# When VectorE transposes the mask of the next chunk in a masked graph attention kernel

## The reference

```python
h = jnp.maximum(_layernorm(x, axis=-1), 0.0)
h1 = h @ a[:d]
h2 = h @ a[d:]
e = leaky_relu(h1 + h2.T, negative_slope=0.01)
attention = softmax(where(adj > 0, e, NEG_BIG), axis=1)
out = x + attention @ h
```

## Time and profile before

| | us |
|---|---|
| median of three runs | 1551.02 |
| lowest, highest | 1548.48, 1551.06 |
| the profiled execution | 1552.08 |
| its span | 1550.3 |
| TensorE matmul, busy | 1522.7 (98%) |
| VectorE, busy | 1489.6 (96%) |
| ScalarE, busy | 1162.5 (75%) |
| GpSimd, busy | 457.4 (30%) |

### The profile page before, as it was taken

How to read it: one execution, slowest core, us unless ns; L and a number is a source line. 1 busy time by engine, 2 the same in 40 slices (tenths; PEclk the granted TensorE clock), 3 DMA queues, 4 the chain that set the end, 5 groups by cost and what they waited for, 6 DMA issues and landing times.

```text
span 1550.3 us, 38852 instructions
## 1 busy us (share of the span) xinstructions
PE 1522.7 (98%) x12678; PEld 1511.9 (98%) x12678; DVE 1489.6 (96%) x2172; ACT 1162.5 (75%) x1180; POOL 457.4 (30%) x547
## 2 busy tenths in 40 slices
PE   5999999999999999999999999999999999999999
PEld 5999999999999999999999999999999999999998
DVE  7999999999999999999999999999999999999998
ACT  7787877778777777677776876777777777677774
POOL 6363334335452340120420320320320320420420
PEclk9999999999999999999999999999999999999999
DMA  6666677787778799999999999999999999999994
GB/s 211 222 200 230 206 223 227 230 248 221 245 220 254 220 225 233 221 201 206 218 207 207 224 204 207 226 197 210 230 195 205 228 195 207 217 195 209 219 199 98
DMA packets 436493, 331.05 MB, mean 214 GB/s; under 512 B 16704, under 2 KB 378176, under 8 KB 436416
## 3 DMA queue, kind: packets, MB, share of 16 engines
q1 hardware_dynamic: 411360, 288.94, 83.6%
q10 hardware_dynamic: 25056, 41.13, 8.7%
HBM read 308.90 MB, written 21.10 MB: 213 GB/s over the span
## 4 chain that ended last, share of the span: by engine, by line
PE 82%; DMA 5%; DVE 3%; ACT 3%; issue 2%; SPq 1%; ACTq 0%; DVEq 0%
PE acc L950 27%; PE acc L953 26%; PE acc L952 26%; DMA adj_in<-in_adj_dram 5%; PE T L917 2%; ACT mask L542 2%; DVE w_lo L797 1%; DVE halves L786 1%; SPq L268 1%; ACT w_hi L552 0%; DVE T L767 0%; DVE w_lo L801 0%; ACT w_hi L555 0%; DVE adj_in L901 0%; DVE adj_in L896 0%
## 5 line engine op out<-in xcount | busy, mean ns | idle before, releaser
L950 PE MATMUL acc<-h_hi,w_hi 128*128 128x258 f32 (+1 forms) x4096 | 1167.3, 285 | 9.2 <-DVE w_lo L801 3.4
L953 PE MATMUL acc<-h_hi,w_lo 128*128 128x258 f32 (+1 forms) x4096 | 1153.3, 282 | 0.0
L952 PE MATMUL acc<-h_lo,w_hi 128*128 128x256 f32 (+1 forms) x4096 | 1149.7, 281 | 0.0
L950 PEld LDWEIGHTS acc<-h_hi,w_hi 128*128 128x128 f32 x4096 | 771.8, 188 | 17.8 <-issue 8.0
L952 PEld LDWEIGHTS acc<-h_lo,w_hi 128*128 128x128 f32 x4096 | 778.4, 190 | 0.1
L953 PEld LDWEIGHTS acc<-h_hi,w_lo 128*128 128x128 f32 x4096 | 775.3, 189 | 0.0
L786 DVE SCALAR_TENSOR_TENSOR halves<-r_rep,g_all,T 128x512 f32<-128x512 f32 (+1 forms) x1024 | 712.7, 736 | 10.8 <-PE T L917 1.5
L542 ACT ACTIVATE mask<-adj_in,mhalf 128x2048 fp8e5<-128x2048 int32 x256 | 510.3, 1993 | 58.8 <-DMA adj_in<-in_adj_dram 58.5
L552 ACT ACTIVATE w_hi<-halves 128x1024 fp32r<-128x1024 f32 x336 | 353.6, 1057 | 185.0 <-DVE halves L786 172.3
L797 DVE SCALAR_TENSOR_TENSOR w_lo<-halves,w_hi 128x1024 fp32r<-128x1024 f32 x336 | 418.2, 1245 | 9.9 <-PE acc L953 4.9
L555 ACT ACTIVATE w_hi<-halves 128x1024 fp32r<-128x1024 f32 x176 | 185.3, 1057 | 97.5 <-DVE halves L786 92.6
(11 more groups left out here) (70 smaller groups left out, 343.8 us busy)
## 6 DMA issues: line engine op xcount, KB each, us to landing
adj_in<-in_adj_dram SPq DMA_DIRECT2D x672, 256.0 KB, 5.0
adj_in<-in_adj_dram SPq DMA_DIRECT2D x88, 1024.0 KB, 6.3
part_sums<-stage ACTq DMA_DIRECT2D x24, 516.0 KB, 5.6
xo<-part_sums ACTq DMA_DIRECT2D x24, 516.0 KB, 4.4
r_rep<-r_rows SPq DMA_DIRECT2D x39, 256.0 KB, 4.8
xb<-in_x_dram ACTq DMA_DIRECT2D x15, 512.0 KB, 5.9
out_dram<-xb ACTq DMA_DIRECT2D x15, 512.0 KB, 4.7
xb<-in_x_dram SPq DMA_DIRECT2D x14, 512.0 KB, 5.8
```

What stands on the lines that cost most here:

```text
L950: nc.tensor.matmul(acc[:, t, 0:WC], w_hi[:, k % HL, cols], rhs_hi, start=start and u == 0, stop=False)
L952: nc.tensor.matmul(acc[:, t, 0:D], w_hi[:, k % HL, cols], rhs_lo, start=False, stop=False)
L953: last = nc.tensor.matmul(acc[:, t, 0:WC], w_lo[:, k % LL, cols], rhs_hi, start=False, stop=stop and u == 1)
```

## The change

On VectorE the transpose of the mask of a chunk moves from the front of the chunk's own work to the chunk before, in front of the weights of its second pair (k = 1 or k = 3), after the subtraction. The condition takes the kind of the chunk that it transposes for: at the end of a visit (`last`, kc = 1) that is `V.dt_next`. The last step of all has no next chunk (`V.tail`). The other engines are untouched.

```diff
-            def transpose_mask(V, n, kc):
+            def transpose_mask(n, kc, dt):
 
                 g = n * CI + kc
-                t = G - V.dt
-                if V.dt < G:
+                t = G - dt
+                if dt < G:
                     dve.wait_ge(s_T, g + 1)
                 else:
                     dve.wait_ge(s_mask, g + 1)
...
                     else:
-                        if V.dt and k % 2 == 0:
-                            transpose_mask(V, n, kc)
                         if not (isinstance(V.v, int) and V.v == 1 and first and k < 2):
                             subtract(g - 2, (k + 2) % 4, True, V.deep and not (enter and k < 2))
+                        dt = V.dt_next if last and kc == 1 else V.dt
+                        if dt and k % 2 == 1 and not (V.tail and last and kc == 1):
+                            transpose_mask(n + (kc + 1) // CI, (kc + 1) % CI, dt)
                         if first:
                             side_work(V, k)
                         if second:
```

## The result

The changed kernel takes 1561.62 us (median of four runs, 1560.06 to 1562.38) against 1549.99 for the kernel before (four runs, 1548.48 to 1551.06). The ratio is 1.0067, 95% interval 1.0052 to 1.0081: slower, by 8 to 13 us. The forecast was slower, 1565, with a range of 1556 to 1577. The profiled spans are 1560.6 and 1550.3.

A forecast was written before the change was run, and what follows sets the result against it. TensorE bounds the kernel, VectorE hardly faster. Three undisturbed pairs of visits (4.2 us) plus five late-load groups (10.0) add 14.2 us to the profiled 1552.1: 1566.3, so 1565 as median; range 1556 to 1577.

The forecast's parts named there:

- The bound, and the lead: TensorE bounds, VectorE catches up 0.2 us per chunk; lead is subtraction's end to its first matmul, 0.45 behind an evacuation.
- (a): Undisturbed chunks: the second weights come 0.63 to 0.65 us later, hidden by VectorE's own work; cost nothing.
- (b): VectorE's mask wait moves ahead of the second weights (1.31 us), delaying them and the next subtraction; 1.22 us behind evacuations.
- The second evacuation, and the pair: Late mask four chunks on the pair's second visit costs 0.48 us; with the first's 0.92, 1.40 per undisturbed pair.
- returns elsewhere: Shared SBUF port: a subtraction's 0.54 us GpSimd slowdown goes at one place, returns at others; under 4 us on the sum.
- The late loads: Conversions waiting for late loads, five groups: each costs TensorE 1.1 to 2.9 us, taken 2.0; 10.0 us in all.
- The low end of the range: Each late-load group 1.1 us, three pairs 4.2: +9.7, down to +5 if loads catch up while TensorE waits.
- The rival of the load queue: SyncE's loads, issued later, bunch less with evacuation transfers; some 12 us regained, 1549; chance of faster 8%.
- one of the two signs of being wrong: VectorE's transpose waits grow but matmul counts don't, or conversions' waits for loads fall well below 57.5 us.
- The ring: Mask, transpose, weights, rounding, conversion form a loop of 5.6 to 6.1 us with scaling; lateness persists, +28, 1579; chance 14%.
- What would show it: VectorE's waits at the transpose go from 6.7 to 35 to 45 us; evacuation stretches lose some 12 matmuls.
- The part up to 560 us: The stretch of the kernel up to 560 us was claimed to stay unchanged.

The follow-up runs named there:

- wait_only: Kernel before, transpose at its old place, but VectorE also waits for the next chunk's mask ahead of the second weights; ratio 1.0066 to the kernel before.
- thin_share: Changed kernel with GpSimd's two operations for empty rows on 8 of 256 columns; ratio 1.0045 to the kernel before.
- light_before: Kernel before with x reload and output store in the last 80 steps cut to one tile of four; ratio 0.9961 to the kernel before, 1545.01 us.
- light_after: Changed kernel with x reload and output store in the last 80 steps cut to one tile of four; ratio 1.0069 to the kernel before, 1561.74 us.
- hold_before: Kernel before with SyncE issuing one load of each eight-step visit 2.2 us later; ratio 1.0031 to the kernel before.
- old_first: Changed kernel with the transpose for the chunk after a visit's first step at its old place; ratio 1.0021 to the kernel before.
- behind_s1: Kernel before with the transpose moved behind the chunk's first subtraction, ahead of its first weights; ratio 1.0093 to the kernel before.

## Why the prediction was right, point by point

The direction and the mechanism were right: the wait ahead of W2 costs, behind the evacuations. That the time came out within 3.4 us of the forecast is partly luck. The forecast added 14.2 us: 4.2 for three undisturbed pairs and 10.0 for late loads. The measured spans differ by 10.3: 5.7 for these pairs, 3.4 for the others and 1.1 ahead of them, which no term foresaw. One term was too small, the other too large by far.

- **The bound, and the lead.** TensorE's pace and VectorE's small reserve were read rightly. The lead of 0.45 of which 0.30 may go gave a stall of 0.92 us behind an evacuation; against the trace before, the chunk behind the evacuation starts 0.93 to 0.95 us later in each of the seven pairs from the second on. The forecast had counted it in three only.
- **(a) W2 later costs nothing.** Right: wait_only leaves undisturbed W2 in place and is as slow, and in the changed kernel the last nine chunks of an undisturbed pair lose nothing with W2 later in each.
- **(b) The wait ahead of W2.** Right, and by wait_only nearly the whole of the cost. Predicted wait of VectorE behind the evacuation 1.22 (from a start that would overlap), listed 1.14; S1 comes 1.21 later.
- **The second evacuation, and the pair.** Predicted 1.40 a pair, measured 1.85 to 1.92. Two steps were off. The second evacuation was priced at 0.48 "with the lead already used"; in the kernel before S1 still had a lead of 0.38 there (over at 883.48, first matmul at 883.86), of which 0.23 could go, and the chunk behind it loses 0.31 to 0.33. The larger one is the slow S. I took it that S1 moves out of GpSimd's way and gains 0.54 a visit. It did, but another S (872.83, 1.70 us) moved into GpSimd's way between the two evacuations, and one behind the second that is slow in both kernels (ten chunks into the pair) now finds less lead (0.41 us; 0.58 in the kernel before). That is the part of the skill's rule that I had set beside the sum ("returns elsewhere"); thin_share, in which all S are quick, shows its price, 0.4 us a pair. Its pairs 3 to 7 lie 1.42 to 1.45 above those of light_before: near 1.40, with other parts than predicted. Three pairs came to 5.7 us instead of 4.2.
- **The late loads.** The term that was mis-sized: 5 x 2.0 = 10.0 us predicted, 3.4 measured (0.8 + 2.2 + 0.9 - 0.8 + 0.3), and these 3.4 hold the evacuations' stalls of the five pairs too. I added the late wait on top of loads as late as before, and let it override the evacuation's 0.92. It was the other way round: the stalls of the evacuations came in every pair from the second on, and covered the loads. The landing was taken to move 0.9 us with its issue, and did (0.6 to 1.2 in the undisturbed pairs); what was not seen is that its use moves further. In the changed kernel ScalarE's conversions after the evacuation come about 2 us later against TensorE (chunk 141: 19.9 us after the start of chunk 136, before 17.9) while the load lands at 16.4 (before 15.7). So the loads are no longer last there. The low end of the range had named this ("if late loads get time to catch up while TensorE waits"). light_before and light_after show it: only the kernel before has anything to gain from fewer bytes.
- **The rivals.** The rival of the load queue had the effect right (waits for loads well below 57.5) and the cause wrong: not loads that bunch less, since a load held back lands later (hold_before), but, as far as the runs show, a backlog that the standstills pay off. It won back some 5 us of the 12 named, not the 10 from which it would have decided. With the fall to 9.7 us one of the two signs of being wrong that the prediction named did appear, and it was right about the part that it concerns: the loads. The ring did not show: the pairs heal within their ten steps, and the leads are those of the kernel before (within 0.05 us) from chunk 147 on, six chunks behind the second evacuation.
- **What would show it.** The waits at the transpose were to be 35 to 45 us, and are 21.0: of the two kinds only the one behind evacuations came in full, fourteen waits in pairs 2 to 8, 1.14 us behind a first evacuation and 0.66 to 0.74 behind a second. Matmuls missing in the stretch with a pair's evacuations: some 12 predicted, 12 measured from 850 to 900 us (422 before, 410 after), 10 from 950 to 1000 (424, 414), and 16 over the whole pair from 954 to 1068.
- **The part up to 560 us** was to be unchanged. Of the 10.3 us of the spans, 1.1 stand there, where the order didn't change. They arise in the first two chunks and stay to 0.1 us for the next 500 us. The six traces with VectorE's old order and no added wait reach the first late chunk at 576.1 to 576.6 us of their spans, six of the eight others at 577.2 to 577.6, the last two at 575.1 and 576.2. It goes with the program more than with the execution; what in it does this is open.

## What to carry to other kernels

A wait in an in-order queue costs what is queued behind it, not what it waits for: before moving a wait ahead of an operation, set the end of what it waits for against the new place chunk by chunk, above all behind the irregular work (here the evacuations), and subtract the lead that the bounding engine still has there. Two causes that stall the same engine don't add up: a stall taken out in one place lets late transfers show in another (old_first), and one put in can hide them (light_before and light_after). So undisturbed periods and sums are to be compared, not single late spots. An operation that could fill time between a writer and its reader is worth its place there even when it seems free to move.

## What the runs showed of the hardware that was not expected

- VectorE starts an operation that reads the result of the one just before it (weights behind the transpose into PSUM that they read, behind_s1) 0.75 us after that one's start in 104 of 168 cases and 0.87 to 0.89 after in the 64 of the hardware loop; an independent one starts 0.63 after (all 168 in the changed kernel, to 0.01). The dependence costs 0.12 us, in the loop 0.25. Over a chunk (5.66 or 5.78 against 5.50, where TensorE needs 5.70) this decided between catching up, keeping up and falling behind.
- A subtraction with both inputs in SBUF was stretched from 1.22 to 1.70 us where a GpSimd operation had begun 0.12 us before it. The same holds over all 14 traces: 273 subtractions that began while a GpSimd tensor_tensor (L410, L419, L426) had more than 0.2 us left took as long as it still ran plus 1.08 us, to 0.03. Where the GpSimd operation had begun at most 0.05 us before the subtraction, it could be the other way round: in 102 cases the subtraction took its usual time and the GpSimd operation 1.5 us or more instead of 0.7. The Trainium skill ("SBUF — State Buffer", section "Who interferes with whom") says that such a VectorE instruction contends with a GpSimd instruction that reads SBUF. The trace agrees for these operations. It shows no such stretch beside L423, a tensor_scalar with its input in SBUF: 306 subtractions began while it was the one running, with more than 0.2 us to go, and the longest took 1.40 us. That operation takes about 1.3 us on 8 columns and 1.5 on 256, and the trace does not show when in that time it reads.
- With the same bytes ahead of it, a load issued later landed later, but not by a fixed amount: issued 2.2 us later it landed 2.7 to 3.1 us later in the three undisturbed pairs of hold_before, and issued 1.8 us later it landed 0.6 to 1.2 us later in the same pairs of the changed kernel, always against TensorE's first matmul of the pair.
